# Turning the attention probabilities by VectorE and DRAM instead of TensorE, with softmax tiles of 4 heads by 32 queries

## The reference, cut

```
q = w_qkv[:4096], k = w_qkv[4096:5120], v = w_qkv[5120:]      # 32 heads, 8 key/value groups, 128 wide
xn = layernorm(x)                                              # x: 1024 tokens x 512
scores = einsum('bskgd,btkd->bkgst', qh, kh) / sqrt(128)
probs = softmax(where(causal, scores, min))                    # over t, 1024 x 1024 a head, lower triangle
attn = einsum('bkgst,btkd->bskgd', probs, vh)
s = attn.reshape(1, 1024, 4096) @ w_dense.T
g = silu(ffn(xn))                                              # three layers of +-1 weights, relu between
return x + s * g
```

## Time and profile before

| | |
|---|---|
| median of 3 runs | 1057.82 us (1057.01 to 1058.14) |
| span of the profiled execution | 1053.9 us |
| PE busy | 1037.8 us (98%) |
| DVE, ACT, POOL busy | 669.0, 520.0, 340.6 us |
| mean DMA rate | 27 GB/s |

### The profile page before, as it was taken

How to read it: one execution, slowest core, us unless ns; L and a number is a source line. 1 busy time by engine, 2 the same in 40 slices (tenths; PEclk the granted TensorE clock), 3 DMA queues, 4 the chain that set the end, 5 groups by cost and what they waited for, 6 DMA issues and landing times.

```text
span 1053.9 us, 17118 instructions
## 1 busy us (share of the span) xinstructions
PE 1037.8 (98%) x5424; PEld 882.4 (84%) x5424; DVE 669.0 (63%) x1454; ACT 520.0 (49%) x1077; POOL 340.6 (32%) x298
## 2 busy tenths in 40 slices
PE   6999999999999999999999999999999999999998
PEld 5888888888888888888888888888888888888886
DVE  8576557756586566765577565865567555666543
ACT  3564446544475445644465444753456444545442
POOL 5242324323143222322143321432323231434533
PEclk9999999999999999999999999999999999999999
DMA  5120001100020001100021000210012000000021
GB/s 189 32 61 11 1 1 51 49 0 0 0 70 30 0 0 33 57 10 0 0 60 40 0 0 0 70 30 0 0 40 56 4 0 0 21 11 1 1 91 60
DMA packets 17015, 28.35 MB, mean 27 GB/s; under 512 B 2144, under 2 KB 3680, under 8 KB 16992
## 3 DMA queue, kind: packets, MB, share of 16 engines
q1 hardware_dynamic: 16992, 28.06, 8.7%
HBM read 25.95 MB, written 2.10 MB: 27 GB/s over the span
## 4 chain that ended last, share of the span: by engine, by line
PE 97%; DVE 2%; DMA 0%; ACT 0%; SPq 0%; issue 0%; ACTq 0%; DVEq 0%
PE ps_m L963 14%; PE ps_m L965 14%; PE ps_m L964 14%; PE ps_t L1013 12%; PE ps_o L965 6%; PE ps_o L963 6%; PE ps_s L965 6%; PE ps_s L964 6%; PE ps_o L964 6%; PE ps_s L963 6%; PE ps_m L1105 3%; PE ps_s L1089 1%; PE ps_m L1061 1%; DVE half_var L784 0%; DMA prob_odd<-x 0%; DVE prob_odd L833 0%
## 5 line engine op out<-in xcount | busy, mean ns | idle before, releaser
L644 POOL TENSOR_TENSOR prob_even<-prob_even,row_inv 128x128 f32<-128x128 f32 (+3 forms) x128 | 135.5, 1070 | 389.5 <-DVE row_inv L819 389.5
L644 POOL TENSOR_TENSOR prob_odd<-prob_odd,row_inv 128x256 f32<-128x256 f32 (+3 forms) x128 | 162.8, 1283 | 276.8 <-DVE row_inv L819 276.8
L716 ACT ACTIVATE pt_hi<-ps_t 128x512 fp32r<-128x512 f32 x288 | 171.3, 598 | 157.9 <-PE ps_t L1013 155.8
L878 DVE TENSOR_TENSOR pt_lo<-ps_t,pt_hi 128x512 fp32r<-128x512 f32 x288 | 197.1, 687 | 72.7 <-ACT pt_hi L716 71.7
L810 DVE CUSTOM_DVE_ANT_0 ps_s<-ps_s,mask 128x128 f32<-128x128 f32 (+7 forms) x256 | 192.9, 766 | 40.5 <-PE ps_s L965 39.8
L963 PE MATMUL ps_m<-xn_hi,w_hi 128*128 128x512 f32 (+1 forms) x376 | 150.4, 400 | 1.3 <-DVE xn_lo L870 0.7
L965 PE MATMUL ps_m<-xn_hi,w_lo 128*128 128x512 f32 (+1 forms) x376 | 147.1, 391 | 0.0
L964 PE MATMUL ps_m<-xn_lo,w_hi 128*128 128x512 f32 (+1 forms) x376 | 147.0, 391 | 0.0
L686 ACT ACTIVATE prob_odd<-ps_s,neg_max 128x256 f32<-128x256 f32 (+3 forms) x128 | 101.6, 795 | 87.9 <-DVE neg_max L810 87.5
L963 PE MATMUL ps_s<-k_hi,q_hi 128*128 128x512 f32 (+5 forms) x384 | 138.8, 361 | 0.0
L965 PE MATMUL ps_s<-k_hi,q_lo 128*128 128x512 f32 (+5 forms) x384 | 131.1, 341 | 0.0
(11 more groups left out here) (108 smaller groups left out, 1598.5 us busy)
## 6 DMA issues: line engine op xcount, KB each, us to landing
raw<-wqkv SPq DMA_DIRECT2D x48, 256.0 KB, 2.6
raw<-wd SPq DMA_DIRECT2D x32, 256.0 KB, 2.6
prob_odd<-x SPq DMA_DIRECT2D x8, 256.0 KB, 4.1
out<-y SPq DMA_DIRECT2D x8, 256.0 KB, 2.0
prob_even<-x SPq DMA_DIRECT2D x7, 256.0 KB, 4.3
raw<-k SPq DMA_DIRECT2D x3, 256.0 KB, 2.8
raw<-x SPq DMA_DIRECT2D x1, 256.0 KB, 2.5
scales<-s SPq DMA_DIRECT2D x3, 0.5 KB, 3.2
```

Source lines behind the costliest of these rows:

```text
L644: pool.tensor_tensor(rows, rows, row_inv[:, slot:slot + 1] .to_broadcast([P, (i + 1) * P]), ALU.mult)\
L716: act.activation(pt_hi[:, t % PT_RING, :, :], ps_t[t % TURN_RING][:, :, :], ACT.Copy).then_inc(turn_hi, 1)
L878: dve.tensor_tensor(pt_lo[:, t % PT_RING, :, :], ps_t[t % TURN_RING][:, :, :], pt_hi[:, t % PT_RING, :, :], ALU.subtract)\
```

## The change

The `turn` items are gone. Instead:

- A softmax tile holds 32 queries of each of the four heads (`Q = 32`, `TILES = 4`), and not 128 queries of one head. Tile r of row block i has (4i+r+1)*32 columns of keys, so that the causal edge is cut at 32 columns. To make the 128 stationary columns of a tile contiguous, `q_hi` and `q_lo` are stored as 32 blocks of 4 heads by 32 queries.
- Three of the four `norm` of a row block move from POOL to ACT.
- `flip`: one DVE instruction a row block transposes all its probabilities in place, in 32x32 blocks, over (i+1)*512 columns.
- `move`: SP waits for the flip, and for some row blocks also until pieces of an SBUF ring (`pt_lo`, 12 slots) are used up, which `LAND_AFTER` lists. It then issues four writes from SBUF to DRAM, one for each 32 partitions, in runs of 512 bytes; waits until all four have landed; and issues one read of (i+1)*256 KB back into `pt_lo`, in runs of 2 KB.
- ACT copies each landed pair (i, j) from SBUF as `pt_hi`, and POOL subtracts in place for `pt_lo`. All low parts of weights move from DVE to POOL too.
- The freed PSUM banks make two banks of `ps_o` and two of `ps_m`.
- SP's list is now planned with the rest, with a constant `MOVE_TIME` of 4.65 us and 2.3 us for the read, whatever i is.

```diff
-                    elif name == "turn":
-                        _, i, j = item
-                        t = tri(i) + j
-                        pe.wait_ge(turn_split, TURNS * g + t + 1)
-                        if j == 0:
-                            pe.wait_ge(normed, SCORES * g + HEADS * (i + 1))
-                        for h in range(HEADS):
-                            mm = pe.transpose(ps_t[t % TURN_RING][:, h, :],
-                                              probs[i % 2][:, h, j * P:(j + 1) * P], ident[:, :])
-                        mm.then_inc(turned, 1)
...
+LAND_AT = [0, 1, 3, 6, 1, 6, 0, 4]
+COLUMNS = [list(range(i + 1)) for i in range(BLOCKS)]
+COLUMNS[6].reverse()
+
+LAND_AFTER = {0: tri(7), 2: 30 - PAIRS, 3: 34 - PAIRS, 4: tri(3), 5: tri(4), 6: tri(5) + 1, 7: tri(6) + 3}
...
+                    if what == "flip":
+                        i, = item
+                        dve.wait_ge(normed_act, NORMS_ACT * r.row_no(i))
+                        if NORMS_ACT < TILES:
+                            dve.wait_ge(normed_pool, (TILES - NORMS_ACT) * r.row_no(i))
+                        dve.transpose(prob_rows(i), prob_rows(i)).then_inc(flipped, 1)
+                        continue
...
+                    elif what == "move":
+                        i, = item
+                        row = i % BLOCKS
+                        sp.wait_ge(flipped, r.row_no(i))
+                        sp.sem_inc(flips_seen)
+                        if kind != "prologue" and row in LAND_AFTER:
+
+                            sp.wait_ge(block_weighed, WEIGHED0 + PAIRS * g + LAND_AFTER[row])
+                        tiles = prob_rows(i).rearrange("p (t c) -> p t c", c=P)
+                        turned = turned_d[i % 2, 0:row + 1, :, :, :, :]
+                        for h in range(HEADS):
+                            sp.dma_start(turned[:, :, :, h, :].rearrange("j b k c -> k (j b) c"),
+                                         tiles[h * Q:(h + 1) * Q, :, :])\
+                              .then_inc(turned_out, 16)
+                        sp.sem_inc(flips_seen)
+                        sp.wait_ge(turned_out, TURNED0 + 16 * HEADS * r.row_no(i))
+                        slots = slice(LAND_AT[row], LAND_AT[row] + row + 1)
+                        sp.dma_start(pt_lo[:, slots, :].bitcast(F32),
+                                     turned.rearrange("j b k h c -> (b k) j (h c)"))\
+                          .then_inc(landed[i % 2], 16)
...
+                    elif what == "lo" and item[0][0] == "land":
+                        _, i, j = item[0]
+                        t = r.pair(i, j)
+                        slot = LAND_AT[i % BLOCKS] + j
+                        hi_slot = 0 if i == BLOCKS else pair_no(i, j) % HI_RING
+                        pool.wait_ge(land_hi, t)
+                        pool.tensor_tensor(pt_lo[:, slot, :], pt_lo[:, slot, :].bitcast(F32),
+                                           pt_hi[:, hi_slot, :], ALU.subtract).then_inc(land_lo, 1)
```

More of the change, by code:

```diff
@@ L48 @@
 RAW = 5
-TURN_RING = 2
-PT_RING = 4
+HI_RING = 4
+LAND = 12
 ATTN_RING = 2
@@ L100, in pe_cost @@
     if kind == "scores":
[L101 to L109, removed]
+        return sum(3 * max(TURN, n / 2400 + 0.014) for _, _, n, _ in score_parts(item[1] % BLOCKS, item[2]))
+    if kind == "vblocks":
+        return 4 * TURN
+    return MATMUL * {"hidden": 2, "final": 2 * CHUNKS}.get(kind, 3)
@@ L112, in plan @@
 def plan(kind, leads):
+    last = kind == "last"
     queues = pe_queues(kind)
-    total = [sum(map(pe_cost, q)) or 1 for q in queues]
+    total = [sum(map(pe_cost, q)) for q in queues]
     done, at = [0.0] * len(queues), [0] * len(queues)
[L119 to L131, removed]
@@ L151, in row @@
[L151 to L159, removed]
@@ new lines, in plan @@
+    for n in range(3 if last else 0):
+        task("sp", ("load", f"k{n}"), 0.47, *([("lo", ("split", splits[n - 1]))] if n else []))
+    def advance(until):
+        while todo:
+            best = None
+            for name, (engine, duration, needs, number) in todo.items():
+                if all(n in end for n in needs):
+                    there = max([end[n] + SIGNAL for n in needs], default=0.0)
+                    if name[0] == "hi" and name[1][0] == "split":
+                        there += LANDS
+                    key = (max(free[engine], there), there, number)
+                    if best is None or key < best[0]:
+                        best = (key, name)
+            if best is None or best[0][0] > until:
+                return
+            (start, _, _), name = best
+            engine, duration, _, _ = todo.pop(name)
+            free[engine] = end[name] = start + duration
+            if name[0] == "move":
+                end[("landed", name[1])] = end[name] + LANDS
+            orders[engine].append(name)
@@ L179, in ready @@
-            return max([bank.get(("score", b), 0.0) for b in score_banks(i, h)]
-                       + [there[("unit", p, half)] for p in ("k", f"q{h}") if i in (0, 4)])
-        if what == "turn":
-            i, j = item[1:]
-            if i and ("norm", i, HEADS - 1) not in there:
-                return None
-            n = tri(i) + j
-            if n >= PT_RING and ("weigh", *pairs[n - PT_RING]) not in end:
-                return None
-            return max(bank.get(("turn", n % 2), 0.0), there.get(("norm", i, HEADS - 1), 0.0))
@@ L230, in ready @@
-        if any(n not in there for n in needs):
-            return None
-        return max([bank.get("shared", 0.0)] + [there[n] for n in needs])
-    pairs = [(i, j) for i in range(BLOCKS) for j in range(i + 1)]
-    splits = [f"wd{n}" for n in range(HEADS)] + ([] if kind == "last" else PIECES)
-    last_split = -9.0
+            i, r = item[1:]
+            if i % 4 == 0 and r == 0:
+                needs += [("lo", ("unit", p, i // 4 % 2)) for p in PIECES if p != "v"]
+            number = TILES * i + r
@@ L306, in plan @@
[L306 to L330 removed]
+                end[w] = t
```

690 lines of the change are left out of this document (379 added, 311 removed).

## The result

The changed kernel takes **1263.0 us** (1261.9 to 1265.3) where the kernel before takes 1057.4 (1056.3 to 1058.1) on the same chip. The ratio is 1.195, with a 95% interval from 1.194 to 1.197: slower by 205.6 us, where 134 were forecast. The profiled execution has a span of 1260.5 us and a time of 1262.2: what lies outside of the first and last instruction is 1.7 us here, so that of the 3.9 us between span and median in the kernel before about half is a difference between executions.

What follows compares the result with a forecast made beforehand. PE's own work was taken to bound the kernel before. For the change, 105.2 + 10.3 + 14.4 + 6 + 3.5 = 139.4 us a group, 16.8 more than 122.6; over eight groups 134 more, so 1192 us, range 1075 to 1290.

Steps and rivals of the forecast that it cites:

- PE's work and the other engines: PE's work falls by 17.4 to 105.2 us a group; DVE, ACT and POOL stay under 105, so none becomes the bound.
- The flip: DVE's 32x32 transposes, priced at 0.54 us for each 512 columns plus 0.15 for the start, 21 us a group.
- Row block 7: Ahead of its first weigh item PE stands 10.3 us a group: the move takes 20.5 us, PE has 10.2 of work.
- Row blocks 3 to 6: PE's stands there, from last score tile to weigh items: 9.1 us for 5 and 6, 5.4 for 3 and 4, together 14.4.
- the small terms: Moves behind weight loads in SP's list and score tiles waiting for an earlier exp: 6 us a group, between 2 and 8.
- The clock: PE's lower clock behind the stands of row block 7 and about row block 6: 3.5 us a group, between 0 and 5.
- The edges: The last group waits less, having feed-forward matmuls to put between, the prologue more; the two were let cancel.
- The rival whose number came up: Writes at 164 GB/s or less because 32 partitions feed them: row block 7 stands 13.7 us, time 1262; chance 0.20.
- The other rivals: Shorter stands, 1006 us (0.10 with about no change); moves wholly hidden, near 930 (0.02); flip at 0.90 us, 1227 (0.06).
- That stands are shorter than 17.4 us a group: Rival: PE's stands stay below the 17.4 us it saves, 116.1 us a group, 1006 us; chance 0.10 with about no change.
- Signs that were named: Changed profile: PE near 75% busy, waits naming POOL's low parts, row block 7's stand some 10 us, then the lower clock.

Runs made afterwards that it cites:

- Warm_fill: The changed kernel with 112 matmuls a group that nobody reads, filling PE's stands ahead of row blocks 3, 5, 6 and 7: 1228.5 us, ratio 1.164.
- no_moves: The changed kernel without the writes to DRAM and the reads back, SP only raising their semaphores: 929.4 us, ratio 0.880.
- late_gate_split: The changed kernel with each move cut in two halves of its columns and the wait for pt_lo slots put before the first read: 1049.3 us, ratio 0.992.
- four_wide_512: The changed kernel with each of the four writes over 128 partitions, runs still 512 bytes, data landing in wrong order: 1181.9 us, ratio 1.118.
- one_write_512: The changed kernel with one write over 128 partitions in place of four, runs still 512 bytes, data landing in wrong order: 1175.5 us, ratio 1.114.
- late_split_fill: late_gate_split with matmuls that nobody reads ahead of row blocks 5 (8), 6 (20) and 7 (16): 1048.9 us against the kernel before, ratio 0.993.

## Why the forecast was right in sign and short in size

**PE's work and the other engines.** Forecast 105.2 us a group, measured 105.2 without moves. DVE, ACT and POOL were to have 66, 79 and 69 us and have 66.2, 73.4 and 66.9. The flip is right to 1%.

**Row block 7.** Forecast 10.3 us, measured 12.4. Writes and read were each priced too cheap, 11.8 us for 10.7 and 8.8 for 7.3, 2.6 us together, and the stand is 2.1 us longer. With its fixed 1.3 us the writes' rate is 2.10 MB in 10.5 us, 200 GB/s and not 225, and the read's, with 1.9, is 304 GB/s and not 390. The 390 came from loads whose source had long lain in DRAM; whether the difference comes from data just written was not tried. (The mean of the one 512-byte burst in the earlier trace rows is 161 GB/s by its 13 slices, not 164, which moves nothing.)

**Row blocks 3 to 6 and the small terms.** Forecast 14.4 and 6; measured 17.7 for row blocks 3 to 6 (3.23 + 0.78 + 5.65 + 7.99) and 1.8 for the rest. All idle time is 31.8 against 30.7: the sum is nearly right, and its parts less so.

**The clock is the term that was mis-sized most.** Forecast 3.5 us a group, between 0 and 5; measured 9.7 of PE's time, outside of these bounds. The step that failed took the one loss of 2.8 us in the earlier trace rows as the size, and counted row block 7 and in part row block 6. But the stands of row blocks 3, 5, 6 and 7 were all followed by PE work at the low level, some 3.5 to 5.5 us of it behind each. (The form of the earlier trace rows is there in the stretch behind row block 6's stand, below.) Warm_fill narrows what it cost: of 7.0 us that PE got back in a group the group became 5.3 shorter, 35 us in the whole. By that share the 9.7 would be worth some 7 us a group (an estimate), still twice the 3.5.

```profile
744.00:749.50 5.50, 5.40 (x13) 4.29 (x14) 0.69 (x1) 2.01 (x4) 5.42 (x6) 0.50 0.00 0
```

Thirteen matmuls in 5.5 us at a clock of 0.50: at the full clock they take 3.0.

**The edges.** The seven groups of the body take 1074.34 - 49.21 = 1025.1 us, 146.4 each on average. SP's queue of the kernel before, first loads of the first and the last group of the body, six groups apart and so 122.6 each:

```profile
60.61 14.64 SPq L586 DMA_DIRECT2D raw<-wd  x4
...
796.08 14.63 SPq L586 DMA_DIRECT2D raw<-wd  x4
```

Each group is longer by 23.9 us on average, 167 in all. The remaining 39 us are in prologue and last group, where 16.8 were forecast and the two were said to cancel. From the first load of the last group the change has 1260.5 - 1074.3 = 186.2 us to go, and no_moves, whose list is the same, 148.0. So the way through DRAM costs the last group 38 us, hardly less than one of the body (41.5): its feed-forward matmuls covered little.

The run without moves shows a second part. Its span is 927.7 us, where 1054 - 8 x 17.4 = 915 had been priced: the body saves 17.2 us a group, but prologue and last group together only some 6 instead of 17.4. The shortfall of the span, 1260.5 - 1188 = 72, is thus 13 us of PE's time that wasn't saved, 7 x (41.5 - 34.2) = 51 for the way in the body, most of it the clock (6.2 a group), and some 9 for the way at the edges. Why PE saves so little at the edges isn't shown.

**The rival whose number came up.** The writes at 164 GB/s or less because 32 partitions feed them had 1262. Its cause is real and large: 81 us hang on the partitions of a write. Its terms are not what was measured: it needed writes of 14.1 us and a stand of 13.7, and they were 11.8 and 12.4. So its number is met partly by chance, with the clock and the last group in place of slower writes. The Trainium skill, page "SBUF — State Buffer", section "Door 1: The DMA port swizzle (why `[64,N]` ≈ `[32,N]`)", has such transfers at 189 GB/s for 1 MiB. The trace is near that: four of them, 2.10 MB, in 11.8 us are 178 GB/s, or 200 behind the fixed 1.3 us; once each write takes 128 partitions it is 8.8 us, 238 and 280 GB/s.

**The other rivals.** That stands are shorter than 17.4 us a group, and so the kernel faster, did not come about by the change, but late_gate_split is that case: 9.9 us of stands and 7.4 of clock are together the 17.4 that PE saves, and it is level with the kernel before. What the forecast had taken as given was the place of the wait for slots: it priced row block 7 from that wait on and did not ask whether the writes needed it.

**Signs that were named.** PE's share near 75% (78%), its waits naming POOL's low parts, the stand of some 10 us, the low clock behind it and the other engines under 70% of the period came as said.

## What to carry to other kernels

Where work moves from a busy engine to a way through DRAM, price the way from the last producer to the first use, not the engines' sums: here PE saved 17.4 us a group and the way took 41.5 back. Ask of every wait on that way which of the steps behind it really needs it, and of every transfer whether the consumer can start on its first half: these two edits to the queue, with no transfer made cheaper, were worth 214 us. Cut a large store so that each part takes all 128 partitions, where the layout allows it, which was not shown here. And where fillers are to hold the clock, look whether each batch ends before the operand behind it is ready.

## What the runs showed of the hardware that was not expected

- Four writes of 2.10 MB in all from 32 partitions each took 11.8 us, from 128 partitions each 8.8, one write 8.7. Four writes cost as little as one, but where they are narrow, they cost 3 us.
- The issue of row block 7's four writes held SP's queue for 5.03 us, where a single one took 0.36. Not each took 1.26: the first two took 0.30 and 0.56, the third and fourth 1.85 and 2.18. For row block 0, a quarter of a megabyte, the four took 1.75 us. With runs of 2 KB, so a quarter of the pieces, the four of row block 7 took 5.2 us, with four wide writes 3.96. It grows with the bytes, then, and not with the pieces. It cost little here: four_wide_512 and one_write_512 are 6 us apart.
- Work at the low clock is not lost in full where PE would stand anyway. In warm_fill fillers gave PE 7.0 us of a group back and the group became 5.3 shorter. In late_split_fill the clock went from 0.963 to 0.987 and the time changed by less than 1 us, but there the fillers themselves held PE up for about 3 us a group, so that nothing about the clock follows from it.
